# A causal and a full attention stage: the row of maxima sent from ScalarE's queue, and PSUM banks shared out two, two and two in place of three, three and one

## The chip, the cores and the metric

The kernel runs on one core of one Trainium2 chip. The metric is the device time of one execution in microseconds (us). TensorE (PE) multiplies, VectorE (DVE) reduces and does element-wise work, ScalarE (ACT) does exponentials and copies out of PSUM, GpSimd (POOL) does element-wise work on SBUF, and SyncE (SP) does nothing but issue DMAs. PSUM has eight banks of 128 partitions by 512 fp32 values.

## The reference

Four layers follow each other on x of shape (8, 512, 128): causal attention with rotary embedding and an output projection, a mixture-of-experts FFN, full attention with rotary embedding, and a dense FFN; each is added to x and followed by a layer norm. Only the two attentions are touched. Cut to what matters:

```python
qkv = x @ Wqkv                                    # 16 heads of 8 values, 512 positions, 8 batches
Q, K = rope(q), rope(k)
scores = einsum('bhqd,bhkd->bhqk', Q, K) / sqrt(8)   # causal in the first attention, full in the second
attn = softmax(scores, axis=-1)                      # exp(score - row maximum) / sum
y = einsum('bhqk,bhkd->bhqd', attn, V)
x = layernorm(x + y @ Wproj)                         # the second attention has no projection
```

## The kernel before, in words

`attention` is called twice. Its work is cut into 32 groups n = 0..31 of four heads (four groups to a batch b = n // 4, t = n % 4), and each group into units u: 12 units in the causal stage (three tiles of four heads), 16 in the full one. In every unit PE does `scores(n, u)` (L505) into a bank `ps_s`, then `maxima(n + 2, u)` (L518) for the group two ahead into a bank `ps_m`, the transposed product from which the row maxima come. Scores and maxima use 25 and 24 of the array's rows, and head i of the scores lies at other rows than the head (i + 2) % 4 of the maxima. ACT takes the exponential of each score unit out of `ps_s` (L433), DVE reduces each unit of maxima out of `ps_m` (L597 causal, L600 full). In odd units PE also does `values` (L533, the product with V), and after four of them in a group `warm` (L459), which multiplies into the bank of the next score unit only to keep PE busy. Small jobs (`job`, L468: transposing x, projecting k, q and v, transposing maxima `maxT`, normalising `norm`, and in the causal stage `yT` and `proj`) stand at fixed units and share the banks `ps_x` in a ring: a job waits until the job that last had its bank has been read.

Banks are numbered in turn: unit g = n * U + u has score bank g % SB and maxima bank g % MB. PE therefore waits in `scores` and `warm` for the exponential SB units back and in `maxima` for the reduction MB units back:

```python
after(pe, s_exp, g - SB + 1)      # scores: unit g; warm: g is the unit after this one
after(pe, s_mx, g - MB + 1)       # maxima
```

The score of a group subtracts the row's maximum through an extra row of the stacked operand `qst`. ACT copies the transposed maxima to `mrow` (L417, once a group, after unit 4 in the causal stage and unit 2 in the full one), and SP sends that row by a DMA into `qst` (`max_row`, L313). `scores(n, 0)` waits for it. SP also sends `stack(b)` (L295), 24 DMAs of 64 KB that build the stacked operands `kst` and `qst` of a batch from `hi_k`, `lo_k`, `hi_q`, `lo_q` (the rotated k and q in two parts, made by POOL, L346 and L352). `maxima(4 * b, 0)` waits for all 24. All queues run in the written order. On SP, stack(b + 1) comes behind the row of group 4b + 1, and the row of group 4b + 2 behind stack(b + 1).

Of the kernel before, what the change touches and what calls it, by code (L numbers as in the profile page):

```python
# [4 lines left out]
F32 = mybir.dt.float32  # L5
# [6 lines left out]
P = 128  # L12
C = 128
B, T = 8, 512
QT = T // P
# [3 lines left out]
NG = H // HG  # L19
PARTS = 3  # L20
QUAD = 32
KROWS = 3 * D
# [212 lines left out]
def attention(nc, sems, x, x_dram, ident, maskw, weights, wproj, cos, sin, tag, ahead=None):  # L235
# [3 lines left out]
    sh = Shapes(causal)  # L239
    U = sh.units  # L240
    G = B * NG
    SB, MB, XB = 3, 3, 1
    START = [("xT", 0), ("k", 0), ("q", 0), ("v", 0), ("xT", 1), ("k", 1), ("q", 1), ("maxT", 0)]
    END = [("norm", G - 1)] + ([("yT", B - 1), ("proj", B - 1)] if causal else [])
    place = sh.ring(START, END, XB)
# [1 line left out]
    with ExitStack() as ctx:  # L247
# [3 lines left out]
        def sbuf(name, shape, dt=F32):  # L251
            return ctx.enter_context(nc.sbuf_tensor(tag + name, shape, dt))


        qst = [sbuf(f"qst{r}", [P, NG, T], F32R) for r in range(2)]
# [10 lines left out]
        mrow = [sbuf(f"mrow{i}", [HG * QT, P], F32R) for i in range(2)]  # L266
# [17 lines left out]
        s_made, s_read, s_swap, s_turn, s_hi, s_lo = sems.made, sems.read, sems.swap, sems.turn, sems.hi, sems.lo  # L284
        s_kst, s_qst, s_mst, s_den, s_res, s_ln = sems.kst, sems.qst, sems.mst, sems.den, sems.res, sems.ln
# [6 lines left out]
        with nc.Block() as block:  # L292
            @block.sync
            def _(sp):
                def stack(b):  # L295

                    r = b % 2
                    if b >= 2:
                        sp.wait_ge(s_score, (b - 1) * NG * U)
                    for name, dst, s_dst, hi_rows, lo_rows in (("k", kst[r], s_kst[r], (D, 2 * D), (0,)),  # L300
                                                               ("q", qst[r], s_qst[r], (0, D), (2 * D,))):
                        sp.wait_ge(s_hi[name], b + 1)
                        for i in range(HG):
                            for row in hi_rows:
                                sp.dma_start(dst[QUAD * i + row:QUAD * i + row + D, :, :].bitcast(F32),
                                             hi[name][QUAD * i:QUAD * i + QUAD, :].bitcast(F32)).then_inc(s_dst, 16)
                        sp.wait_ge(s_lo[name], b + 1)
                        for i in range(HG):
                            for row in lo_rows:
                                sp.dma_start(dst[QUAD * i + row:QUAD * i + row + D, :, :].bitcast(F32),  # L310
                                             lo[name][QUAD * i:QUAD * i + QUAD, :].bitcast(F32)).then_inc(s_dst, 16)

                def max_row(n):  # L313

                    b, t = divmod(n, NG)
                    sp.wait_ge(s_read["maxT"], n + 1)
                    sp.dma_start(qst[b % 2][KROWS:P:QUAD, t, :].bitcast(F32).rearrange("i (j q) -> i j q", j=QT),
                                 mrow[n % 2][:, :].bitcast(F32)).then_inc(s_mst, 16)

                if causal:  # L320
                    for b in range(B):
                        sp.dma_start(x[:, QT * b:QT * b + QT, :], x_dram[b]).then_inc(s_load[b], 16)
                sp.wait_ge(s_ones, 2)
                stack(0)
                max_row(0)
                if ahead is not None:
                    ahead(sp)
                for n in range(G):
                    if n + 1 < G:
                        max_row(n + 1)  # L330
                    if n % NG == 0 and n // NG + 1 < B:
                        stack(n // NG + 1)

            def rope(eng, b, name, step):

# [20 lines left out]
            def _(pool):  # L356
# [9 lines left out]
                def hide(n, j):  # L366

                    k, (col, _) = sh.tile_of[j], sh.piece_of[j]
                    pool.wait_ge(s_exp, n * U + (k + 1) * HG)
                    diag = prob[k][:, :, col:col + P]  # L370
                    pool.affine_select(out=diag, in_=diag, compare_op=ALU.is_ge, fill=0.0, base=0,  # L371
                                       pattern=[[0, HG], [1, P]], channel_multiplier=-1).then_inc(s_mask, 1)
# [19 lines left out]
            @block.scalar  # L392
            def _(act):
                def read_out(name, n):

                    act.wait_ge(s_made[name], n + 1)
                    ps_x = ps_j[place[name, n][0]]
                    if name == "xT":
                        if n:
                            act.wait_ge(s_made["v"], n)  # L400
                        ins = act.activation(xT[:, :], ps_x[:, :], ACT.Copy)
                    elif name in "kq":
                        if n:
                            act.wait_ge(s_swap[name], n)
                            act.wait_ge(s_turn[name], 3 * n)
                        ins = act.activation(raw[name][:, :], ps_x[:, :], ACT.Copy)
                    elif name == "v":
                        if n < 2:
                            act.wait_ge(s_vinit, 4)
                        else:  # L410
                            act.wait_ge(s_pv, (n - 1) * NG * QT)
                        ins = act.activation(vst[n % 2][:, :, :, 0:D],
                                             ps_x[:, :].rearrange("p (j h d) -> p j h d", j=QT, h=H), ACT.Copy)
                    elif name == "maxT":
                        if n >= 2:
                            act.wait_ge(s_mst, (n - 1) * 16)
                        ins = act.activation(mrow[n % 2][:, :], ps_x[0:HG * QT, 0:P], ACT.Copy, scale=-1.0)  # L417
                    else:
                        assert name == "yT"
                        if n:  # L420
                            act.wait_ge(s_made["proj"], n)
                        ins = act.activation(yT[:, :], ps_x[:, :], ACT.Copy)
                    ins.then_inc(s_read[name], 1)

                def exponentials(n, u):

                    k, i = divmod(u, HG)
                    g = n * U + u
                    w = sum(w for _, _, w in sh.score[k])
                    act.wait_ge(s_score, g + 1)  # L430
                    if i == 0 and n:
                        act.wait_ge(s_pv, sh.tile_free(n - 1, k))
                    act.activation(prob[k][:, i, 0:w], ps_s[g % SB][:, 0:w], ACT.Exp, scale=float(D) ** -0.5)\  # L433
                        .then_inc(s_exp, 1)

                def out_read(n):

                    act.wait_ge(s_pv, (n + 1) * QT)
                    if n:
                        act.wait_ge(s_made["norm"], n)  # L440
                    act.activation(oT[:, :], ps_o[:, :], ACT.Copy).then_inc(s_oT, 1)  # L441

                for name, n in START:
                    read_out(name, n)
                for n in range(G):
                    for u in range(U):
                        exponentials(n, u)
                        if u == sh.out_at and n:
                            out_read(n - 1)
                        for name, m in sh.behind(n, u, 1):  # L450
                            if name not in ("norm", "proj"):
                                read_out(name, m)
                out_read(G - 1)
                if causal:
                    read_out("yT", B - 1)
# [1583 lines left out]
```

## Time and profile before

| | us |
|---|---|
| median of 3 runs (lowest, highest) | 1502.93 (1495.87, 1503.41) |
| the profiled execution | 1501.69 |
| its span, first to last instruction | 1500.0 |
| PE busy in the span | 1239.8 (83%) |
| DVE, ACT, POOL busy | 921.8, 788.9, 521.6 |
| mean granted TensorE clock | 0.891 of 2.4 GHz |

The causal stage lies between about 14 and 480 us of the span, the full one between about 720 and 1210. PE's instructions run in order and several matmuls on different rows of the array can be under way at once, so a busy PE is not PE at its peak. Where PE is the engine that the others wait for, a wait of PE moves the end by as much.

### The profile page before, as it was taken

The page shows a single profiled execution, that of the slowest core. Times are in us where ns is not written, and L with a number is a line of the kernel's source. Part 1 is how long each engine was busy: PE and PEld are TensorE (multiplying, and loading weights), DVE is VectorE, ACT ScalarE, POOL GpSimd, SP SyncE. Part 2 cuts the span into 40 slices and gives each one's busy share as a digit, 9 for nine tenths or more (in the row PEclk, how much of TensorE's full clock was granted, in tenths as well). Part 3 has the DMA queues.
Part 4 walks back from the last instruction along what each step waited for, and adds up shares of the span by engine and source line. Part 5 has one row for each costly group of instructions (what it writes and reads, how often), then busy time and mean ns, then how long its engine had stood idle before and what let it go on. Part 6 is the DMA issues. An engine that isn't in the chain of part 4 may idle for free. (4 is left out here: it accounts for less than half of the span.)

```text
span 1500.0 us, 28689 instructions
## 1 busy us (share of the span) xinstructions
PE 1239.8 (83%) x10443; PEld 726.8 (48%) x10443; DVE 921.8 (61%) x2838; ACT 788.9 (53%) x1543; POOL 521.6 (35%) x476
## 2 busy tenths in 40 slices
PE   3588977877798597794399899899898969999996
PEld 1344434434454464672144344343343447888885
DVE  3556855866673766445388788788787642334542
ACT  1144644644554663443137676676676745556553
POOL 3324523532511455573513033033030004445553
PEclk9988977988878598897559899999999989999998
DMA  4212113202300401333340310310321000000000
GB/s 101 29 39 45 28 18 44 34 13 44 44 2 2 130 15 41 109 62 66 42 108 15 44 34 12 44 36 11 44 31 15 2 15 8 15 14 14 14 21 15
DMA packets 55948, 53.26 MB, mean 36 GB/s; under 512 B 8000, under 2 KB 38720, under 8 KB 55824
## 3 DMA queue, kind: packets, MB, share of 16 engines
q1 hardware_dynamic: 51808, 48.33, 16.2%
q0 software_dynamic: 3696, 2.76, 1.3%
q8 instruction: 77, 1.26, 0.4%
q14 instruction: 47, 0.39, 0.1%
q10 hardware_dynamic: 320, 0.52, 0.1%
HBM read 15.74 MB, written 8.06 MB: 16 GB/s over the span
## 5 line engine op out<-in xcount | busy, mean ns | idle before, releaser
L433 ACT ACTIVATE a_prob<-a_ps_s 128x512 f32<-128x512 f32 (+1 forms) x896 | 466.4, 565 | 340.3 <-PE a_ps_s L514 336.1
L600 DVE TENSOR_REDUCE a_mx<-a_ps_m 128x1 f32<-128x512 f32 x512 | 327.9, 682 | 87.7 <-PE a_ps_m L529 86.3
L529 PE MATMUL a_ps_m<-a_kst,a_qst 24*128 24x512 f32 (+3 forms) x1024 | 284.1, 480 | 43.8 <-DMA a_qst<-a_lo_q 36.8
L597 DVE CUSTOM_DVE_ANT_0 a_junk<-a_ps_m,maskw 128x384 f32<-128x384 f32 (+3 forms) x512 | 227.2, 486 | 148.6 <-PE a_ps_m L529 148.5
L514 PE MATMUL a_ps_s<-a_qst,a_kst 25*128 25x512 f32 (+3 forms) x1024 | 246.4, 464 | 76.9 <-DMA a_qst<-a_mrow 67.4
L551 PE MATMUL a_ps_o<-a_prob,a_vst 128*32 128x256 f32 (+2 forms) x3840 | 286.6, 387 | 2.9 <-ACT a_oT L441 2.1
L514 PEld LDWEIGHTS a_ps_s<-a_qst,a_kst 25*128 25x128 f32 x1024 | 110.9, 193 | 230.8 <-ACT a_prob L433 95.7
L371 POOL TENSOR_SCALAR_AFFINE_SELECT a_prob<-a_prob 128x512 f32<-128x512 f32 x128 | 80.1, 638 | 265.6 <-ACT a_prob L433 265.6
L465 PE MATMUL a_ps_s<-a_kst 128*32 128x256 f32 x2000 | 169.8, 414 | 0.0
L529 PEld LDWEIGHTS a_ps_m<-a_kst,a_qst 24*128 24x128 f32 x1024 | 129.1, 200 | 72.1 <-issue 40.4
L551 PEld LDWEIGHTS a_ps_o<-a_prob,a_vst 128*32 128x32 f32 x3840 | 86.8, 113 | 106.4 <-issue 71.2
L338 POOL TENSOR_TENSOR a_rot_k<-a_rot_k,sin_table 128x512 f32<-128x512 f32 x16 | 20.5, 1279 | 286.3 <-DVE a_rot_k L608 286.3
L1698 POOL TENSOR_TENSOR f_hid_lo<-f_gelu_h,f_hid_hi 128x512 fp32r<-128x512 f32 x64 | 83.2, 1300 | 101.1 <-ACT f_hid_hi L1661 101.1
L1736 PE MATMUL f_ps_h<-f_hid_hi,f_h_hi 128*128 128x512 f32 x256 | 103.4, 404 | 4.0 <-POOL f_hid_lo L1698 4.0
L1738 PE MATMUL f_ps_h<-f_hid_lo,f_h_hi 128*128 128x512 f32 x256 | 101.4, 396 | 0.0
L1737 PE MATMUL f_ps_h<-f_hid_hi,f_h_lo 128*128 128x512 f32 x256 | 100.6, 393 | 0.0
L1698 POOL TENSOR_TENSOR f_hid_lo<-f_gated_h,f_hid_hi 128x512 fp32r<-128x512 f32 x32 | 41.5, 1298 | 154.7 <-ACT f_hid_hi L1650 153.9
L465 PEld LDWEIGHTS a_ps_s<-a_kst 128*32 128x32 f32 x2000 | 68.7, 119 | 35.4 <-issue 7.3
L1833 DVE SCALAR_TENSOR_TENSOR f_u<-f_th,f_ps_a 128x512 f32<-128x512 f32 x32 | 21.8, 683 | 56.3 <-ACT f_th L1645 56.3
L1736 PEld LDWEIGHTS f_ps_h<-f_hid_hi,f_h_hi 128*128 128x128 f32 x256 | 48.6, 190 | 15.8 <-POOL f_hid_lo L1698 6.4
L1738 PEld LDWEIGHTS f_ps_h<-f_hid_lo,f_h_hi 128*128 128x128 f32 x256 | 48.6, 190 | 11.2
L1737 PEld LDWEIGHTS f_ps_h<-f_hid_hi,f_h_lo 128*128 128x128 f32 x256 | 48.7, 190 | 10.0
(292 smaller groups left out, 1933.2 us busy)
## 6 DMA issues: line engine op xcount, KB each, us to landing
a_kst<-a_hi_k SPq DMA_DIRECT2D x128, 64.0 KB
a_qst<-a_hi_q SPq DMA_DIRECT2D x128, 64.0 KB
f_w<-in_L_ffn_W_dram SPq DMA_DIRECT2D x21, 256.0 KB, 3.6
a_kst<-a_lo_k SPq DMA_DIRECT2D x64, 64.0 KB
a_qst<-a_lo_q SPq DMA_DIRECT2D x64, 64.0 KB
x_tiles<-in_L_attn_x_dram SPq DMA_DIRECT2D x8, 256.0 KB, 4.6
normed_rows_dram<-f_nrm SPq DMA_DIRECT2D x8, 256.0 KB, 2.3
f_hT_hi<-expert_sums_dram SPq DMA_DIRECT2D x4, 512.0 KB, 6.0
```

What stands on the lines that cost most here:

```text
L371: pool.affine_select(out=diag, in_=diag, compare_op=ALU.is_ge, fill=0.0, base=0, pattern=[[0, HG], [1, P]], channel_multiplier=-1).then_in ...
L433: act.activation(prob[k][:, i, 0:w], ps_s[g % SB][:, 0:w], ACT.Exp, scale=float(D) ** -0.5)\
L465: pe.matmul(ps_s[g % SB][VW * i:VW * i + VW, 0:2 * P], kst[r][:, t, VW * i:VW * i + VW].bitcast(F32), kst[r][:, t, 0:2 * P].bitcast(F32), ...
L514: last = pe.matmul(ps_s[g % SB][:, col:col + w], kst[r][lo_row:end, t, P * j:P * j + P], qst[r][lo_row:end, t, T - w:T], start=True, stop= ...
L529: last = pe.matmul(ps_m[g % MB][:, col:col + w], qst[r][lo_row:end, t, P * j:P * j + P], kst[r][lo_row:end, t, 0:w], start=True, stop=True)
L551: last = pe.matmul(ps_o[VW * i:VW * i + VW, end - w:end], vst[b % 2][:, j, HG * t + i, :], prob[k][:, i, col + at:col + at + w], start=(j ...
L597: ins = dve.tensor_tensor_reduce(junk[g % MB][:, col:col + w], bank[:, col:col + w], maskw[:, T - w:T], 1.0, -3.0e38, ALU.add, ALU.max, out)
L600: ins = dve.reduce_max(out, bank[:, col:col + w], AX.X)
L1698: pool.tensor_tensor(dst, src[:, :], hi.bitcast(F32), ALU.subtract).then_inc(s_lo, 1)
L1736: pe.matmul(out, w_hi[w][:, k, cols], hi, start=start, stop=False)
L1737: pe.matmul(out, w_lo[w][:, k, cols], hi, start=False, stop=False)
L1738: return pe.matmul(out, w_hi[w][:, k, cols], lo, start=False, stop=stop)
```

## The change

The DMA of the row of maxima is issued by ACT, right behind ACT's copy that makes it, in place of SP. The wait in front of it, for ACT's own copy, moves with it. SP's queue then holds only loads and stacks, so stack(b + 1) follows stack(b) and its own waits. The seven banks beside `ps_o` are shared out as 2 for scores, 2 for maxima and 2 for small jobs (six in all), in place of 3, 3 and 1. Work and order on PE, DVE and POOL are otherwise the same.

```diff
-    SB, MB, XB = 3, 3, 1
+    SB, MB, XB = 2, 2, 2
...
-                def max_row(n):
-
-                    b, t = divmod(n, NG)
-                    sp.wait_ge(s_read["maxT"], n + 1)
-                    sp.dma_start(qst[b % 2][KROWS:P:QUAD, t, :].bitcast(F32).rearrange("i (j q) -> i j q", j=QT),
-                                 mrow[n % 2][:, :].bitcast(F32)).then_inc(s_mst, 16)
...
                 stack(0)
-                max_row(0)
                 if ahead is not None:
                     ahead(sp)
-                for n in range(G):
-                    if n + 1 < G:
-                        max_row(n + 1)
-                    if n % NG == 0 and n // NG + 1 < B:
-                        stack(n // NG + 1)
+                for b in range(1, B):
+                    stack(b)
...
                     ins.then_inc(s_read[name], 1)
+                    if name == "maxT":
+                        b, t = divmod(n, NG)
+                        act.wait_ge(s_read["maxT"], n + 1)
+                        act.dma_start(qst[b % 2][KROWS:P:QUAD, t, :].bitcast(F32).rearrange("i (j q) -> i j q", j=QT),
+                                      mrow[n % 2][:, :].bitcast(F32)).then_inc(s_mst, 16)
```

What stood in SP's queue before, in the causal stage (`kst` and `qst` are the stacked operands, `mrow` the row of maxima, x8 a run of eight DMAs):

```order
L317 DMA a0_qst1<-a0_mrow0 4x4x128
L317 DMA a0_qst1<-a0_mrow1 4x4x128
L305 DMA a0_kst0<-a0_hi_k 8x4x512 x8
L310 DMA a0_kst0<-a0_lo_k 8x4x512 x4
L305 DMA a0_qst0<-a0_hi_q 8x4x512 x8
L310 DMA a0_qst0<-a0_lo_q 8x4x512 x4
L317 DMA a0_qst1<-a0_mrow0 4x4x128
L317 DMA a0_qst1<-a0_mrow1 4x4x128
```

And what stands there after:

```order
L305 DMA a0_kst1<-a0_hi_k 8x4x512 x8
L310 DMA a0_kst1<-a0_lo_k 8x4x512 x4
L305 DMA a0_qst1<-a0_hi_q 8x4x512 x8
L310 DMA a0_qst1<-a0_lo_q 8x4x512 x4
L305 DMA a0_kst0<-a0_hi_k 8x4x512 x8
L310 DMA a0_kst0<-a0_lo_k 8x4x512 x4
```

Before, the third row of a batch stood behind the 24 DMAs of the next batch's stack, and that stack behind the second row. No row is left on SP.

What stood in ACT's queue before, from the last units of a group to the copy of the row (`prob` is the exponential, `ps_s0` to `ps_s2` the score banks):

```order
L433 ACTIVATE a0_prob0<-a0_ps_s0 128x512 [waits a_pv,a_score]
L433 ACTIVATE a0_prob0<-a0_ps_s1 128x512 [waits a_score]
L433 ACTIVATE a0_prob0<-a0_ps_s2 128x512 [waits a_score]
L433 ACTIVATE a0_prob0<-a0_ps_s0 128x512 [waits a_score]
L433 ACTIVATE a0_prob1<-a0_ps_s1 128x512 [waits a_pv,a_score]
L417 ACTIVATE a0_mrow1<-a0_ps_x0 16x128 [waits a_mst,a_made_maxT]
```

And after:

```order
L427 ACTIVATE a0_prob0<-a0_ps_s0 128x512 [waits a_pv,a_score]
L427 ACTIVATE a0_prob0<-a0_ps_s1 128x512 [waits a_score]
L427 ACTIVATE a0_prob0<-a0_ps_s0 128x512 [waits a_score]
L427 ACTIVATE a0_prob0<-a0_ps_s1 128x512 [waits a_score]
L427 ACTIVATE a0_prob1<-a0_ps_s0 128x512 [waits a_pv,a_score]
L406 ACTIVATE a0_mrow1<-a0_ps_x1 16x128 [waits a_mst,a_made_maxT]
L416 DMA a0_qst1<-a0_mrow1 4x4x128 [waits a_read_maxT]
L427 ACTIVATE a0_prob1<-a0_ps_s1 128x512 [waits a_score]
```

The score banks repeat after two units, the small jobs have banks `ps_x0` and `ps_x1`, and the DMA stands between the copy and the exponential of the next unit.

## Rows read from the trace of the kernel before

**Rows 1.** The waits: engine, line, releaser; us in total, times, longest.
```profile
ACT a_prob L433 <- PE a_ps_s L514: 336.1, 311, 12.3
PEld a_ps_s L514 <- ACT a_prob L433: 95.7, 207, 0.8
PE a_ps_s L514 <- DMA a_qst<-a_mrow: 67.4, 14, 7.2
```
**Rows 2.** The timeline of SP in batch 2: start, us, line, DMAs in a run.
```profile
172.82 5.69 SPq L305 DMA_DIRECT2D a_kst<-a_hi_k  x8
...
189.90 37.47 SPq L317 DMA_DIRECT2D a_qst<-a_mrow  x4
```
**Rows 3.** The timeline of PE: the first scores behind the wait of that batch.
```profile
198.41 0.79 PE L514 MATMUL a_ps_s<-a_qst,a_kst 25*128 25x512 f32 x1 [7.18 <-DMA a_qst<-a_mrow]
```
**Rows 4.** Windows: stretch, length, busy PE, PEld, DVE, ACT, POOL; PEclk, DMA share, GB/s.
```profile
155.00:160.00 5.00, 3.63 (x48) 1.49 (x38) 3.53 (x13) 1.72 (x5) 0.89 (x2) 1.00 0.00 0
187.00:188.00 1.00, 1.00 (x9) 0.46 (x13) 1.00 (x7) 0.00 (x0) 0.64 (x1) 0.50 0.52 68
196.00:197.00 1.00, 0.00 (x0) 0.00 (x0) 0.00 (x0) 0.00 (x0) 0.00 (x0) 0.50 0.31 27
203.00:204.00 1.00, 1.00 (x11) 0.19 (x4) 1.00 (x6) 0.44 (x1) 0.49 (x1) 0.59 0.00 0
```
**Rows 5.** The timeline of ACT: copies of the row of maxima, and the exponential behind one.
```profile
171.91 0.25 ACT L417 ACTIVATE a_mrow<-a_ps_x 16x128 fp32r<-16x128 f32 x1
181.46 0.25 ACT L417 ACTIVATE a_mrow<-a_ps_x 16x128 fp32r<-16x128 f32 x1
181.62 0.57 ACT L433 ACTIVATE a_prob<-a_ps_s 128x512 f32<-128x512 f32 x1
205.02 0.25 ACT L417 ACTIVATE a_mrow<-a_ps_x 16x128 fp32r<-16x128 f32 x1
```
**Rows 6.** The timeline of PE in the causal stage, first units of a group.
```profile
158.09 0.49 PE L514 MATMUL a_ps_s<-a_qst,a_kst 25*128 25x512 f32 x1
159.20 0.61 PE L465 MATMUL a_ps_s<-a_kst 128*32 128x256 f32 x8
159.74 0.49 PE L514 MATMUL a_ps_s<-a_qst,a_kst 25*128 25x512 f32 x1
160.42 0.61 PE L465 MATMUL a_ps_s<-a_kst 128*32 128x256 f32 x8
```
**Rows 7.** The timeline of ACT and DVE in the same stretch.
```profile
158.61 0.60 ACT L433 ACTIVATE a_prob<-a_ps_s 128x512 f32<-128x512 f32 x1 [3.28 <-PE a_ps_s L514]
158.76 0.69 DVE L597 CUSTOM_DVE_ANT_0 a_junk<-a_ps_m,maskw 128x512 f32<-128x512 f32 x1 [1.44 <-PE a_ps_m L529]
159.37 0.08 DVE L597 DVE_READ_ACCUMULATOR2_ANT a_mx<- 128x1 f32 x1
159.37 0.69 DVE L597 CUSTOM_DVE_ANT_0 a_junk<-a_ps_m,maskw 128x512 f32<-128x512 f32 x1
```
**Rows 8.** The timeline of PE in the full stage: warming and bare pairs.
```profile
860.72 0.49 PE L514 MATMUL a_ps_s<-a_qst,a_kst 25*128 25x512 f32 x1
861.61 0.61 PE L465 MATMUL a_ps_s<-a_kst 128*32 128x256 f32 x8
...
869.18 0.50 PE L514 MATMUL a_ps_s<-a_qst,a_kst 25*128 25x512 f32 x1
...
870.18 0.50 PE L514 MATMUL a_ps_s<-a_qst,a_kst 25*128 25x512 f32 x1
```
**Rows 9.** The timeline of SP: the first row's DMA alone.
```profile
61.92 0.57 SPq L317 DMA_DIRECT2D a_qst<-a_mrow  x1
```
**Rows 10.** The timeline of POOL: `hi_k` and `hi_q` of batch 3.
```profile
166.06 1.27 POOL L346 TENSOR_TENSOR a_hi_k<-a_full_k,a_rot_k 128x512 fp32r<-128x512 f32 x1
175.71 1.28 POOL L346 TENSOR_TENSOR a_hi_q<-a_full_q,a_rot_q 128x512 fp32r<-128x512 f32 x1
```
**Rows 11.** Groups of instructions: one of the small jobs.
```profile
L481 PE MATMUL a_ps_x<-a_xT,heads_k 128*128 128x512 f32 x32 | 21.7, 765 | 10.0 <-DVE a_y L620 6.9 <-ACT a_xT L401 3.1
```

## What the change was predicted to do

> **What bounds the kernel now.** I read the waits first, then the timelines of SP, PE, ACT and DVE around the longest wait, and the windows for the clock. In both attention stages ACT waits 336.1 us for PE's scores, while PE's own long waits are few [rows 1]. So PE sets the pace, and each delay of PE there counts in full. One kind of wait stands out: PE waits 14 times, 67.4 us in all, for the row of maxima [rows 1]. It comes once a batch. In batch 2 SP issues the stack from 172.82, gets to the row at 189.90, and PE goes on at 198.41 after 7.18 us idle [rows 2, 3]. Traffic goes on until about 197 [rows 4], so the row waited for SP's 17 us of issuing and then behind the stack's data in the queue. ACT had made the row at 181.46 [rows 5]. The clock makes it dearer: it stands at 0.50 (1.2 GHz) from 187 and is back at 2.4 GHz only within 203 to 204 [rows 4]. From copy to copy of the row a group takes 9.55 us (171.91 to 181.46), but the one with the wait takes 23.56 (to 205.02) [rows 5].
>
> The other thing to see is how tightly PE and ACT mesh even with three banks: the weight load of a score unit stands 207 times, 95.7 us in all, in front of an exponential that isn't done, never over 0.8 us [rows 1]. The spare bank isn't idle.
>
> **Term 1, the row's own wait: a gain of 57 us.** The row leaves ACT at about 181.7 + 0.6 in batch 2, 10 us before PE wants it at 191.23 (198.41 less 7.18). Its wait goes. What is late next is the stack: the maxima of group 4b + 2 wait for all 24 DMAs. Their data ended at about 197, and the stack began at 172.82. In the changed kernel it begins when hi_k is there and the last batch's scores are done, at about 167.4 (166.06 + 1.27 [rows 10]), 5.4 us earlier. Its second half needs hi_q, ready at 176.99 [rows 10]. 24 DMAs took 21.5 us of traffic (from about 175), so 12 take 10.8; the first twelve are through at about 180, the last at about 191 and their signal a us or two later. PE comes at 191.2, so 1.5 us is left of a wait of 7.18 in a causal batch. In the full stage groups are longer and little is left. I take 7 x 1.5, some 10 us, off 67.4. The bounds are 0 left (gain 67) and 1.8 us of each gained (5.4 less 3.6, half the head start lost to hi_q: gain 25).
>
> **Term 2, the slow clock behind these waits: a gain of 19 us.** The group with the wait took 23.56 us; with its extra v job it should take 10.6 (9.55 [rows 5] and an estimated 1.1 for the job). Of the 13.0 lost, 7.2 are the wait [rows 3] and 5.8 the slow running around it. There are seven such batches in the causal stage, most with somewhat less: 38 us at 5.4 each. Bounds: 0 (the clock falls anyway: in batch 2 it was down at 187 [rows 4], before the wait began at 191) and 38. I take the middle. In the full stage, where the clock is up until the wait starts, I count nothing.
>
> **Term 3, two banks for small jobs: a gain of 9 us.** A job then waits for the reader of the job before last. The 6.9 us of the k projection behind DVE's normalising [rows 11] and some 2 us of shorter ones go. In the start-up, where a job waits 0.7 us for each read-out, the stack's DMAs follow anyway. Bounds 3 to 13.
>
> **Term 4, two score and two maxima banks: a loss of 117 us.** The unit of work on PE is a pair of units: four matmuls (scores and maxima of both) start within 0.02 us of each other, since they lie at different rows of the array, and take 0.43 us before the next kind starts. Take a causal pair that starts at 158.09. Its first exponential starts at 158.61 and takes 0.60 [rows 7], so the bank is free 1.17 after the pair's start (0.52 + 0.60 + 0.05). ACT's next follows 0.48 later, and frees its bank at 1.65. DVE's first reduction starts at 158.76, the second at 159.37, and that ends at 0.69 + 0.08 more [rows 7]: second maxima bank free at 2.05 to 2.1.
> With three banks the warming unit waits for none of these. With two it waits for the first exponential of its own pair, the next first score for the same one, the next second score for the second exponential, and the next second maxima for the second reduction.
> - Warming (four a group in either stage) starts 1.11 after the pair in one case and 0.68 in the next (159.20 and 160.42 against 158.09 and 159.74) [rows 6]. In place of that 1.2: losses 0.1 and 0.5. The third of a causal group stands behind as much `values` work as the first but shorter columns (an estimated 0.3), the fourth behind exponentials of half the width (0). Together 0.9. In the full stage all four are like 861.61 against 860.72, 0.89 [rows 8]: 0.3 each, 1.2.
> - Second reduction: the next pair follows at 1.66 (159.74) [rows 6], after the loss above at about 1.75 to 2.0, and its second maxima may start only at 2.05. A pair without warming is the worse: 1.00 from 869.18 to 870.18 [rows 8]. There the first maxima wait until 1.3, the second until 1.9. The pair is then staggered by 0.6, no longer four at once, and the next values and warming come later by as much. That is 0.9 for a bare pair, one a causal group (with a 0.3 at the group's end where the normalising stands before DVE's last reduction), one or two a full group. 0.9 + 0.3 less what overlaps with the first item gives 1.0 in the causal stage; 1.0 in the full one, where a job in the pair covers the stagger in half of them.
> Together 1.9 a group causal, 2.0 full (1.2 + 1.0 less 0.2 for pairs with a long job), over 30 groups each: 57 + 60 = 117 us. Bounds: 45 us where only warming and half of it counts (0.75 a group), and 165 us at 2.75 a group with every stagger passed on.
>
> **Term 5, the DMA on ACT: a loss of 30 us.** The next exponential starts 0.16 after ACT's copy (181.46, 181.62) [rows 5]. Now the copy must end (0.25, and 0.05 for the signal) and the DMA be issued; on SP one took 0.57 [rows 9]. The trace shows no such DMA on ACT beside exponentials. The next exponential starts about 0.7 later (0.27 + 0.57 less 0.16). It is the second of its pair, whose bank with two banks is waited for: free at about 2.4 instead of 1.65. Of this 0.7 about 0.5 isn't covered by term 4, 60 times: 30 us. Bounds: 0 (ACT gets so far ahead that nobody waits) and 42. Queued behind it are the exponentials, and for them PE waits.
>
> Sum: 1501.7 for the profiled execution - 57 - 19 - 9 + 117 + 30 = 1563.7. The profiled execution lies 1.2 us under the median of 1502.93, so the forecast of the median is 1565 us, 4.1% slower.
>
> **Rivals.**
> - A, faster: the third banks are a reserve that the pair's rhythm doesn't need. Place: the pairs of every group. It speaks for it that no wait for an exponential is over 0.8 us [rows 1] and that ACT is idle between its pairs. Then terms 4 and 5 are at their lower ends, 45 and 0: 1501.7 - 57 - 38 - 9 + 45 = 1444. It decides once the banks cost under 1.4 us a group (85 / 60). Against it: the 207 waits, and the exponential's end at 1.17 is later than three of four warmings.
> - B, the clock: each pair now has a PE gap of 0.3 to 0.5 us. In 155 to 160 PE was busy 3.63 of 5 us and the clock stayed at 1.00; in batch 2 it was down at 187, four us before the long idle time began [rows 3, 4]. So it stands near the edge, and groups of 9.6 us with 2.4 more idle may go over it. At 1.2 GHz the same matmul took 0.79 instead of 0.49 [rows 3, 6], so a pair of 1.66 takes 2.65 or so. Against the new 1.9 that is 0.75 more; in 60 of the 180 causal pairs 45 us, and term 2 is lost: 1565 + 45 + 19 = 1629.
> - C, the wait moves: the stack lands no earlier than PE wants it, since hi_q and the queue hold its second half. Term 1 is then 25 and term 2 zero: 1565 + 32 + 19 = 1616. It speaks against it that the causal groups get longer, which gives the stack 4 us more.
> The Trainium skill, "TensorE: Matmul & The Clock Gate", section "A second HAM failure mode: psum-queue depth-cycling", tells of a kernel that cycled through PSUM banks and whose short gaps made the clock swing between its two levels. By that, rival B is what would happen here; the trace bears it out only so far as the clock that was down at 187.
>
> **How the numbers follow.** Forecast 0.5, A 0.17, B 0.18, C 0.15. The forecast's own range, with one of the large terms at half its distance to a bound, is 1525 to 1600. A range for 8 in 10 leaves out the better half of A and the worst of B: 1470 to 1630. A measurement of this kernel tells about 0.5% (7.5 us) from no change. Faster by more: A but for its tail, and a bit of the forecast's, 0.15; within: 0.05; slower: 0.80.
>
> **What the changed profile would show.** Right: no wait of PE for the row; a wait of the maxima for lo_q of 0 to 3 us in causal batches only; SP's stacks from about 5 us earlier; waits for exponentials and reductions in hundreds, PE's before warming and second maxima; copies of the row 11.5 to 12 us apart where they were 9.55; the exponential behind the copy 0.8 us after it. Wrong: spacing still near 9.6 (A), PEclk at 0.50 away from the batch's end (B), maxima waiting 4 us or more for lo_q (C). A spacing that grows in the causal stage but not in the full one would make the term of the bare pairs wrong.

## The result, and the profile after

The changed kernel is slower by 10%: 1653.47 us (median of 4 runs, 1644.02 to 1661.73) against 1500.82 us of the kernel before (4 runs, 1495.87 to 1503.41) on the same chip. The ratio is 1.1019, 95% interval 1.0941 to 1.1098. The prediction was 1565 us with a range of 1470 to 1630. The direction was right, and the loss was two and a half times the one forecast. Where times and ratios stand side by side below, a time is the median of all executions, and a ratio leaves out one execution each of runs 3 and 5 that took over 1.5% longer than the fastest of the same kernel.

The page of the changed kernel, its first part and the clock line:
```profile
PE 1398.4 (84%) x10443; PEld 764.5 (46%) x10443; DVE 939.0 (57%) x2838; ACT 807.7 (49%) x1543; POOL 521.3 (31%) x476
...
PEclk8588887889876888985599889888797857999998
```
The matmuls are the same 10443 as before, but PE is busy for 1398.4 us where it was 1239.8, 13% more. Part of that is slower running: the score matmuls take 497 ns on average instead of 464, and the clock line has 8s and 7s also in the second attention stage (slices 21 to 32), where before most slices stood at 9. The other part is that matmuls which used to run at the same time now start one after another (windows of 7 and 8 below); busy time counts them apart.

Next the waits of the changed kernel (columns as in [rows 1]):
```profile
ACT a_prob L427 <- PE a_ps_s L508: 439.4, 427, 10.4
...
PEld a_ps_s L508 <- ACT a_prob L427: 150.8, 262, 1.2
...
PE a_ps_m L523 <- DMA a_qst<-a_lo_q: 51.7, 2, 26.6
PEld a_ps_s L459 <- ACT a_prob L427: 51.1, 139, 0.6
PE a_ps_s L508 <- ACT a_prob L427: 49.7, 91, 0.9
...
PEld a_ps_m L523 <- DVE a_mx L594: 38.6, 71, 1.5
...
PE a_ps_s L508 <- DMA a_qst<-a_mrow: 6.6, 2, 4.3
```
The row's wait is gone but for the start of the two stages: 67.4 us in 14 waits [rows 1] have become 6.6 in 2. In its place stand hundreds of waits, none long, of score and warming units for exponentials and of maxima for reductions. The weight load alone waits 150.8 us for exponentials (95.7 before, [rows 1]). The maxima wait for `lo_q` only at the two stage starts, and longer there than before (51.7 us for 36.8).

The stack of batch 3 in SP's timeline, and ACT's copies 9 to 11 (counted from 0) with what stands behind one:
```profile
181.85 6.87 SPq L305 DMA_DIRECT2D a_kst<-a_hi_k  x8
```
```profile
187.94 0.25 ACT L406 ACTIVATE a_mrow<-a_ps_x 16x128 fp32r<-16x128 f32 x1
188.22 0.54 ACTq L416 DMA_DIRECT2D a_qst<-a_mrow  x1
188.81 1.09 ACT L427 ACTIVATE a_prob<-a_ps_s 128x512 f32<-128x512 f32 x2 [0.62 <-ACT a_mrow L406]
...
200.67 0.25 ACT L406 ACTIVATE a_mrow<-a_ps_x 16x128 fp32r<-16x128 f32 x1
...
216.85 0.25 ACT L406 ACTIVATE a_mrow<-a_ps_x 16x128 fp32r<-16x128 f32 x1
```
The stack begins 6.1 us before copy 9, the second one of the batch under way; before, it began 0.9 us after that copy (172.82 against 171.91, [rows 2, 5]). The exponential stands 0.87 behind the copy's start, where it was 0.16 [rows 5]. The group from 200.67 to 216.85 takes 16.18 us where it took 23.56. Groups without a batch's end take longer: 11.68 (176.26 to 187.94) against 9.65, and 12.73 against 9.55. The first of these two runs at full clock, the second at a mean of 0.87.

Last, windows (columns as in [rows 4]). First the kernel before: its full stage, from the copy of row 0 to that of row 31, and its causal stage from 100 us on:
```profile
763.29:1187.46 424.17, 392.33 (x4092) 169.80 (x4092) 352.28 (x757) 289.62 (x569) 76.12 (x60) 0.94 0.20 35
...
100.00:464.75 364.75, 306.32 (x3672) 165.08 (x3672) 244.18 (x1142) 188.19 (x422) 145.04 (x172) 0.86 0.19 28
```
And of the changed kernel: the full stage, the causal stage from 100 us, two single groups of the full stage, a piece of the first of them, and the 33 us behind the full stage's last copy:
```profile
803.54:1330.70 527.16, 485.77 (x4091) 194.52 (x4091) 362.79 (x757) 301.50 (x570) 75.95 (x60) 0.85 0.14 21
...
100.00:494.02 394.02, 360.49 (x3753) 176.52 (x3751) 250.89 (x1158) 196.83 (x429) 145.18 (x173) 0.85 0.16 26
...
1086.60:1105.65 19.05, 18.10 (x145) 7.51 (x141) 12.55 (x31) 10.04 (x20) 0.04 (x1) 0.73 0.53 70
1105.65:1121.07 15.42, 13.35 (x137) 5.64 (x133) 12.40 (x33) 9.57 (x19) 0.00 (x0) 1.00 0.01 3
...
1089.00:1092.00 3.00, 3.00 (x26) 0.89 (x18) 1.43 (x3) 1.94 (x4) 0.00 (x0) 0.50 0.54 71
...
1330.70:1364.00 33.30, 32.98 (x204) 11.57 (x196) 1.10 (x4) 16.17 (x31) 0.00 (x0) 0.50 0.01 1
```
By stage, the span grew by some 157 us: 3 before the first copy, 26 in the causal stage, 11 between the stages, 103 in the full stage, 15 behind it. The full stage is where the forecast failed most. It holds clean groups of 15.4 us at full clock (the second of the two) beside groups of 17 to 20 us; in the first of the two the clock averages 0.73, so for half its time it was at 0.50 (1.2 GHz). Between 1089 and 1092 PE looks 100% busy. It isn't doing more, each matmul takes longer:
```profile
1086.76 0.49 PE L508 MATMUL a_ps_s<-a_qst,a_kst 25*128 25x512 f32 x1
...
1088.12 0.50 PE L508 MATMUL a_ps_s<-a_qst,a_kst 25*128 25x512 f32 x1 [0.74 <-ACT a_prob L427]
...
1089.06 1.10 PE L459 MATMUL a_ps_s<-a_kst 128*32 128x256 f32 x8
1090.09 0.79 PE L508 MATMUL a_ps_s<-a_qst,a_kst 25*128 25x512 f32 x1
```
This is PE's timeline in the group whose row was copied at 1086.60. A score unit waits 0.74 us for the exponential that ACT's DMA had delayed, and within a microsecond of that wait the warming unit takes 1.10 where it took 0.61, and the score matmul 0.79 in place of 0.50.

The trace records the granted clock as a list of stretches. Its first entry lies at 77 us of the span in the kernel before, at 24 in the changed one, so stretches are added up from 100 us of the span to its end: at 0.50 stand 27 stretches with 318 us before, and 56 with 473 us after.

### The profile page after: what moved, and what is told of

Same layout as the page of the kernel before. It is cut to its first block and busy times, and to the rows that moved or that the text cites. A ratio compares the mean times of both kernels' runs of the same rounds, so it can differ in the third digit from the quotient of the medians.

```text
span 1657.9 us, 28687 instructions
## 1 busy us (share of the span) xinstructions
PE 1398.4 (84%) x10443; PEld 764.5 (46%) x10443; DVE 939.0 (57%) x2838; ACT 807.7 (49%) x1543; POOL 521.3 (31%) x476
## 5 line engine op out<-in xcount | busy, mean ns | idle before, releaser
L427 ACT ACTIVATE a_prob<-a_ps_s 128x512 f32<-128x512 f32 (+1 forms) x896 | 475.2, 568 | 464.4 <-PE a_ps_s L508 439.4
L594 DVE TENSOR_REDUCE a_mx<-a_ps_m 128x1 f32<-128x512 f32 x512 | 338.1, 687 | 184.8 <-PE a_ps_m L523 184.0
L523 PE MATMUL a_ps_m<-a_kst,a_qst 24*128 24x512 f32 (+3 forms) x1024 | 361.4, 502 | 72.2 <-DMA a_qst<-a_lo_q 51.7
L508 PE MATMUL a_ps_s<-a_qst,a_kst 25*128 25x512 f32 (+3 forms) x1024 | 310.5, 497 | 59.5 <-ACT a_prob L427 49.7
L545 PE MATMUL a_ps_o<-a_prob,a_vst 128*32 128x256 f32 (+2 forms) x3840 | 319.2, 424 | 0.0
L508 PEld LDWEIGHTS a_ps_s<-a_qst,a_kst 25*128 25x128 f32 x1024 | 134.8, 204 | 266.5 <-ACT a_prob L427 150.8
L523 PEld LDWEIGHTS a_ps_m<-a_kst,a_qst 24*128 24x128 f32 x1024 | 156.6, 207 | 112.7 <-issue 53.3
L459 PE MATMUL a_ps_s<-a_kst 128*32 128x256 f32 x2000 | 186.0, 449 | 9.8 <-ACT a_prob L427 4.4
L459 PEld LDWEIGHTS a_ps_s<-a_kst 128*32 128x32 f32 x2000 | 60.2, 123 | 87.6 <-ACT a_prob L427 51.1
L486 PE MATMUL a_ps_x<-ident,a_oT 128*128 128x128 f32 x256 | 52.6, 340 | 1.6 <-ACT a_oT L435 1.6
```

Source lines behind the costliest of these rows:

```text
L459: pe.matmul(ps_s[g % SB][VW * i:VW * i + VW, 0:2 * P], kst[r][:, t, VW * i:VW * i + VW].bitcast(F32), kst[r][:, t, 0:2 * P].bitcast(F32), ...
L508: last = pe.matmul(ps_s[g % SB][:, col:col + w], kst[r][lo_row:end, t, P * j:P * j + P], qst[r][lo_row:end, t, T - w:T], start=True, stop= ...
L523: last = pe.matmul(ps_m[g % MB][:, col:col + w], qst[r][lo_row:end, t, P * j:P * j + P], kst[r][lo_row:end, t, 0:w], start=True, stop=True)
L545: last = pe.matmul(ps_o[VW * i:VW * i + VW, end - w:end], vst[b % 2][:, j, HG * t + i, :], prob[k][:, i, col + at:col + at + w], start=(j ...
L594: ins = dve.reduce_max(out, bank[:, col:col + w], AX.X)
```

## The experiments

Each ratio is to runs of the kernel before on the same chip (median 1498.71 us for 1 to 4, 1495.75 for 5 to 8, 1498.93 for 9 and 10). "Low clock" is the sum of the stretches at 0.50 from 100 us on, in the profiled execution; those of 3 and 5 were the longest of their four (1570.51 and 1615.25 us). "Banks s, m, x" are the score, maxima and small-job banks.

| | banks | row issued by | time, us | ratio (95%) | low clock, us |
|---|---|---|---|---|---|
| before | 3,3,1 | SP | 1500.82 | 1 | 318 |
| 1 | 3,3,1 | ACT | 1449.93 | 0.9682 (0.9645 to 0.9719) | 210 |
| 2 | 2,2,2 | SP | 1630.00 | 1.0900 (1.0856 to 1.0944) | 413 |
| 3 | 3,2,2 | ACT | 1552.98 | 1.0343 (1.0268 to 1.0418) | 333 |
| 4 | 2,3,2 | ACT | 1577.66 | 1.0559 (1.0501 to 1.0616) | 340 |
| 5 | 2,2,2 and one for warming | ACT | 1600.28 | 1.0667 (1.0612 to 1.0723) | 398 |
| 6 | as 5, more warming | ACT | 1575.10 | 1.0513 (1.0472 to 1.0555) | 227 |
| 7 | 2,2,2 | GpSimd | 1597.18 | 1.0691 (1.0642 to 1.0740) | 333 |
| 8 | 3,3,1 | GpSimd | 1434.79 | 0.9591 (0.9527 to 0.9656) | 221 |
| 9 | 2,2,1 | ACT | 1649.28 | 1.1018 (1.0966 to 1.1071) | 446 |
| 10 | 3,3,1, half stack held | GpSimd | 1429.75 | 0.9506 (0.9468 to 0.9544) | 235 |
| after | 2,2,2 | ACT | 1653.47 | 1.1019 (1.0941 to 1.1098) | 473 |

**1: the moved row alone.** The changed kernel with
```
-    SB, MB, XB = 2, 2, 2
+    SB, MB, XB = 3, 3, 1
```


> The row's DMA on ScalarE's queue as in the changed kernel, banks 3, 3, 1 as before. Theory (the banks are the loss, the moved row a gain): PE's 14 waits for the row (67 us) go, some slow clock with them, and ACT's DMA is hidden by the third bank, so 1420 to 1460 us, ratio to before about 0.96, copies of the row 9.5 to 10 us apart in the causal stage. Rival (the DMA on ScalarE's queue is the loss): 1530 us or more, since its 0.7 us stands in all 64 groups and the stack's wait takes the place of the row's.

1449.93 us, as the theory had it: this half of the change is a gain of 49 us. The rows of the full stage, and two of its copies, one group apart:
```profile
720.34:1137.71 417.37, 392.08 (x4092) 164.92 (x4092) 353.81 (x757) 290.11 (x570) 76.08 (x60) 0.96 0.18 28
```
```profile
949.88 0.25 ACT L406 ACTIVATE a_mrow<-a_ps_x 16x128 fp32r<-16x128 f32 x1
...
963.01 0.25 ACT L406 ACTIVATE a_mrow<-a_ps_x 16x128 fp32r<-16x128 f32 x1
```
The clock holds at 0.96. The group takes 13.13 us; the same one took 12.52 before. So ACT's DMA costs 0.6 a full group even with three banks.

**2: the banks alone.** The kernel before with the same line at 2, 2, 2.

> Banks 2, 2, 2 as in the changed kernel, the row's DMA on SyncE's queue as before. Theory: the waits for the row stay (14, about 60 us) and the banks cost their full price, so slower than the changed kernel: 1680 to 1720 us. Rival (the DMA on ScalarE's queue is the loss): 1530 to 1580, faster than the changed kernel's 1653.

1630.00, between the two theories. The banks alone cost 131 us, and with them the row's move loses 23 where with three it gains 49: the edits don't add. One reason stands in the waits of this kernel:
```profile
PE a_ps_s L514 <- DMA a_qst<-a_mrow: 12.3, 5, 2.9
```
PE waits less for the row where groups are longer; of 67.4 us [rows 1] only 12.3 are left to be gained. The other reason is what ACT's DMA costs between two banks (7).

**3 and 4: one bank given back.** The changed kernel with `SB, MB, XB = 3, 2, 2`, and with `2, 3, 2`.

> The changed kernel with a third score bank (3, 2, 2). Theory: warming and the second score unit no longer wait for the pair's own exponentials and the DMA on ScalarE is covered, but the maxima still wait for the reduction two units back. I put 60 per cent of the banks' price on the score bank: about 1530 us. Rival (the maxima bank is the dear one): 1600 or more.

> The changed kernel with a third maxima bank (2, 3, 2). Theory: the second maxima and the stagger behind them no longer wait, 40 per cent of the banks' price comes back: about 1570 us, with waits for exponentials as in the changed kernel. Rival (the maxima bank is the dear one): 1510 or less.

1552.98 and 1577.66. From the changed kernel, a third score bank gives 100 us and a third maxima bank 76, of the 203 that lie between 1 and the changed kernel. Each result lies nearer its theory (1530, 1570) than its rival. Both kinds matter, the scores more.

**5 and 6: warming in a bank of its own, and then more of it.** The warming matmuls' result is never read; in 5 they go to the eighth, free bank and wait for nothing:
```
-                    after(pe, s_exp, g - SB + 1)
...
-                        pe.matmul(ps_s[g % SB][VW * i:VW * i + VW, 0:2 * P], kst[r]...
+                        pe.matmul(ps_v[VW * i:VW * i + VW, 0:2 * P], kst[r]...
```
6 adds warming units in front of the small jobs, one a causal group and four a full one:
```
+                        if u in ((7,) if causal else (3, 7, 11, 15)) and (n, u) != (G - 1, U - 1):
+                            warm(n, u)
```


> The changed kernel, with the warming matmuls going to the eighth bank, which the changed kernel leaves free, so that they wait for no exponential; same work. Theory: my 0.9 us (causal) and 1.2 us (full) a group for the warming's wait come back in part, since the second maxima then wait instead; about 30 to 50 us of 1653, so 1605 to 1625, and the waits of the warming for exponentials vanish. Rival (all that counts is the second reduction): no change, 1645 to 1660.

> As the run before, with more warming matmuls in the spare bank: also in the pairs that had none (unit 7 in the causal stage, units 3, 7, 11 and 15 in the full one), 8 more instructions of some 0.55 us in all each time, 150 times. Theory (the clock's falls make up the rest of the loss): falls of the clock go from 58 to 25 or fewer and, as the added work lies in gaps, the time is 20 us or more under the run before, 1590 or less. Rival (the waits alone make up the loss, the clock does little): the added work of 0.55 x 150 = 80 us is half hidden and the time is 30 us or more over the run before.

1600.28 and 1575.10. No wait of warming for an exponential is left in 5, and the time is 53 us lower, just under the expected range. The full stage of 5, then of 6:
```profile
778.48:1287.20 508.72, 466.84 (x4091) 196.57 (x4091) 363.22 (x757) 300.86 (x569) 76.02 (x60) 0.88 0.15 22
```
```profile
755.33:1260.12 504.79, 475.95 (x5055) 213.83 (x5059) 364.86 (x757) 301.13 (x570) 76.02 (x60) 0.96 0.15 23
```
6 runs 964 more matmul records in that stage and is still shorter. The clock there goes from 0.88 to 0.96, and the low stretches of the whole kernel from 398 us in 47 stretches to 227 in 23 (473 in 56 in the changed kernel). The profiled execution of 5 was its longest, but its four executions were granted 0.858 to 0.877 and those of 6 0.909 to 0.914, so the difference doesn't hang on it. The gaps between the pairs pull the clock down, and filling them brings it back. This is the run that shows the clock as a cause and not a by-product: only the filler was added, and it can't shorten a group by itself. At full clock it costs: the cleanest four groups of the full stage take 15.48, 15.15, 15.56 and 15.36 us in 5 and 16.76, 16.18, 15.97 and 15.95 in 6, some 0.8 more each, or 26 us over 31 groups. The stage is 4 us shorter all the same, so by this estimate about 30 us came back from the clock there.

**7 and 8: the row on GpSimd.** The DMA is taken out of ACT's small job and issued by POOL, once a group, with a semaphore of its own in each attention; 7 has banks 2, 2, 2 and 8 has 3, 3, 1:
```
+                def max_row(n):
+                    b, t = divmod(n, NG)
+                    pool.wait_ge(s_read["maxT"], n + 1)
+                    pool.dma_start(qst[b % 2][KROWS:P:QUAD, t, :]..., mrow[n % 2]...).then_inc(s_mst, 16)
```


> The changed kernel with the row's DMA issued by GpSimd in place of ScalarE, banks 2, 2, 2. Theory (the DMA holds up the second exponential of a pair, and with two banks that is passed on): 0.5 to 0.6 us a group over 62 groups and the clock falls that go with it, 30 to 60 us: 1595 to 1625. Rival (the DMA on ScalarE costs nothing): 1645 to 1660.

> Banks 3, 3, 1 with the row's DMA issued by GpSimd. With the row on ScalarE the full stage's groups were 13.1 and 13.7 us apart instead of 12.5 and 13.1. Theory: that 0.6 us goes in about 60 groups, 25 to 37 us: 1412 to 1425, and the groups are 12.5 and 13.1 apart. Rival (GpSimd gets to its DMA late, behind its rotations and masks): waits for the row come back and the time is 1450 or more.

1597.18, as the theory had it, and 1434.79, over the expected 1412 to 1425, though the groups are 12.5 and 13.1 apart as forecast. ACT's DMA costs 56 us with two banks and 15 with three; the 15 is the weaker number, since the intervals of 1 and 8 overlap a little, but the full stage of 8 (400.93 us against 417.37) and its groups (12.54 against 13.13) say the same. With two banks the profiled executions are 69 us apart, and 51 of these lie in the full stage, whose row in 7 reads:
```profile
793.85:1270.18 476.33, 454.59 (x4091) 190.49 (x4091) 360.58 (x757) 299.48 (x569) 93.97 (x91) 0.93 0.16 24
```
against 527.16 at 0.85 with ACT's DMA. The pair 7 and 8 also gives the cleanest price of the banks. The copies of one full group in 8, and of one in 7:
```profile
944.56 0.25 ACT L416 ACTIVATE a_mrow<-a_ps_x 16x128 fp32r<-16x128 f32 x1
...
957.10 0.25 ACT L416 ACTIVATE a_mrow<-a_ps_x 16x128 fp32r<-16x128 f32 x1
```
```profile
1052.29 0.25 ACT L416 ACTIVATE a_mrow<-a_ps_x 16x128 fp32r<-16x128 f32 x1
...
1067.22 0.25 ACT L416 ACTIVATE a_mrow<-a_ps_x 16x128 fp32r<-16x128 f32 x1
```
12.54 and 14.93, so 2.4 us for this group; the causal groups between copies 8 and 9 took 9.66 and 11.65, 2.0 more. The windows of these two full groups, 8 and then 7, and of one more in 7:
```profile
944.56:957.10 12.54, 12.40 (x141) 6.08 (x141) 11.69 (x30) 9.67 (x21) 6.94 (x6) 1.00 0.54 70
```
```profile
1052.29:1067.22 14.93, 14.58 (x145) 6.73 (x141) 12.46 (x31) 9.98 (x20) 6.93 (x6) 1.00 0.54 70
882.54:897.38 14.84, 13.54 (x137) 5.83 (x133) 12.30 (x33) 9.49 (x20) 0.58 (x1) 1.00 0.16 20
```
All three run at full clock. In the same group PE is busy for 14.58 us instead of 12.40, though its matmuls average 0.40 us in both: they no longer run side by side. So a busy PE hides the gaps of the pairs.

**9: the second small-job bank.** The changed kernel with `SB, MB, XB = 2, 2, 1`.

> The changed kernel with one bank for the small jobs in place of two, all else as in it. It isolates the prediction's third term (9 us gained by the second bank, bounds 3 to 13). Theory: a job on one bank waits for the read-out of the job before, and PE idles some tenths of a us for it now and then; this kernel then takes 1656 to 1670 us, the changed one beside it 1653. Rival: with two score and two maxima banks PE waits for those anyway, and the third term's waits are hidden behind them, so that nothing changes: within 3 us of 1653, or even less if the longer queue of small jobs had made the exponentials late.

1649.28: no difference from the changed kernel (1.1018 against 1.1019). The rival was right, the second bank is worth nothing beside two score and two maxima banks. With three of each it would need a ninth bank.

**10: the first row ahead of the stack.** 8 with
```
                         sp.wait_ge(s_hi[name], b + 1)
+                        if b == 1 and name == "q":
+                            sp.wait_ge(s_read["maxT"], 1)
```


> Three score, three maxima and one small bank with the row of maxima issued on GpSimd (1435 us before), and in addition the second half (q) of batch 1's stack waits until the first row has been made, at about 62 us. Theory: at the start the first row waited for data of that stack which was in flight ahead of it (issued 62.6, PE went on at 73.4 after 6.9 us idle); with the half stack issued behind it the row lands within 2 to 3 us of its issue, PE's wait for it at the start falls from 6.9 to about 0, group 1 comes some 7 us earlier, and the stack is complete at about 75, just in time: 1425 to 1430 us. Rival 1: the wait only moves to the maxima of batch 1, which then find the stack late by as much: 1435. Rival 2: the row's own DMA takes 9 us there for another reason: PE's wait stays near 6.9.

PE's first scores of the causal stage in 8, and in this kernel:
```profile
73.41 0.79 PE L513 MATMUL a_ps_s<-a_qst,a_kst 25*128 25x512 f32 x1 [6.88 <-DMA a_qst<-a_mrow]
```
```profile
66.06 0.79 PE L515 MATMUL a_ps_s<-a_qst,a_kst 25*128 25x512 f32 x1
```
The wait is gone, and PE is 7.35 us earlier though GpSimd issued the row at the same moment (62.57 and 62.62). The next copy follows the first by 8.45 us and not 15.6. The rows show that much. They don't show a faster kernel: the last causal copy stands at 422.38 us against 422.73, and the profiled executions took 1438.72 and 1437.97, so the 7 us were lost again on the way, with 48 us of low clock in the causal stage instead of 31. The median, 1429.75, is in the expected range, but the intervals of 8 and 10 overlap a little. It is the lowest time here, 4.9% under the kernel before; that it beats 8 isn't shown.

## Why the prediction was wrong

**The step that failed** is the treatment of the clock. Term 2 says of the full stage, "where the clock is up until the wait starts, I count nothing", and terms 4 and 5 were priced from matmuls and gaps at full clock. By stage, the terms and what the two profiled executions show:

| | predicted | measured |
|---|---|---|
| causal stage | -31 - 19 - 7 + 57 + 15 = +15 | +26 |
| full stage | -26 - 2 + 60 + 15 = +47 | +103 |
| outside both | 0 | +29 |

Of the full stage's excess of 56, most is slow running. The four groups of a batch, each at its cleanest (clock 1.00 from copy to copy; some shorter groups near the stage's start and end left out), take:

| full stage, us a group | groups of a batch | mean |
|---|---|---|
| run 8 (banks 3,3,1) | 12.93, 13.12, 12.52, 13.25 | 12.96 |
| run 7 (banks 2,2,2) | 15.15, 15.35, 14.93, 14.84 | 15.07 |
| changed kernel (and DMA on ACT) | 15.78, 15.38, 15.55, 15.42 | 15.53 |

The 14.84 is the window from 882.54 shown in 7; the other groups in that place take 16.0 to 16.1 in run 7, with the clock down for part of them. So at full clock the banks cost 2.1 us a group and ACT's DMA 0.46, where the prediction had 2.0 and 0.5: 66 and 14 us over the stage's 31 groups, beside the forecast 60 and 15. 31 groups of 15.53 would be 481 us, and they took 527, so 46 us are an estimate of what the falls of the clock cost there. With the 23 us that the stage gains from the moved row (run 8 against the kernel before) that is the whole of it: -23 + 66 + 14 + 46 = 103. By the trace's list of stretches the stage was at 0.50 for 55 us before and for 158 us after. Behind the stage, the last window shows 33 us at 0.50 where the kernel before stood at 0.90; from the last copy to the end it lost 15 us. Between the stages the kernels take 298.5 us (before), 301.5 (run 1), 306.9 (run 2) and 309.5 (changed), so most of the 11 us comes with the banks.

Rival B had this mechanism, with 0.18, but priced it in the causal stage alone. There low clock rose little in sum (104 to 116 us, from 100 us on), but it is other low clock: the moved row takes most of the old stretches away (24 us left in run 1), and the banks bring new ones (102 in run 7). By the rule of the Trainium skill that the prediction cited ("TensorE: Matmul & The Clock Gate", "A second HAM failure mode: psum-queue depth-cycling") the clock was to swing, and the traces agree (27 stretches, then 56); the page tells it of a bf16 kernel and gives no size.

Term by term, in medians, in the order row, banks, ACT, from runs 8, 7 and the changed kernel:

| | predicted | measured |
|---|---|---|
| row off SP's queue (terms 1 and 2) | -76 | -61 (1495.8 to 1434.8) |
| second small-job bank (term 3) | -9 | 0 (run 9) |
| two score and two maxima banks (term 4) | +117 | +162 (1434.8 to 1597.2) |
| DMA on ACT (term 5) | +30 | +56 (1597.2 to 1653.5) |

The misses are 15 + 9 + 45 + 26 = 95 us, less 7 because the kernel before ran at 1495.8 beside runs 7 and 8: the 88 between 1565 and 1653. In another order the parts read otherwise: banks +131, row -33, ACT +56.

**Terms 1 and 2** held in mechanism. The wait for the row went, the stack started early, no maxima of a batch waited for it. By the profiles of the kernel before and run 8 the causal stage gains 42 us (forecast 50), the full one 23 (26), and 3 are lost between them. Of the 8 missing in the causal stage, 7 lie in its first group, where the row now waits behind the stack (15.60 us against 8.45).

**Term 3** was mis-sized. The 6.9 us that PE waited before the k projection [rows 11] are gone in run 9 too, with one small-job bank, so the two score and maxima banks cover them. At the stage starts the second bank only moves a wait: PE waits 51.7 us for `lo_q` with it and 38.5 without.

**Term 4** was right at full clock: 2.1 us a full group for the 2.0, and 2.0 for the 1.9 in the causal group that can be compared. By the profiles of 8 and 7 the stages grow by 61 us (causal, predicted 57) and 75 (full, 60, of which 66 at full clock). That the causal 61 comes so near is partly luck, since it holds slow running that the term left out (102 us of low clock for 31). So with the spacing: copies that were 9.65 apart are 11.68 apart, in the forecast 11.5 to 12, but those that were 9.55 apart, which the forecast named, are 12.7 to 14.3 apart, at a clock of 0.87 or 0.76. Another 17 us lie outside the stages, where no term was, and the last 9 between these profiled executions and the medians. One small piece that the working left out: DVE's last step of the layer norm stands ahead of reductions, and with two banks PE waits for them (22 waits for reductions in the full stage, 12.0 us in all). In the full stage of the changed kernel, DVE and then PE:
```profile
1115.28 1.11 DVE L72 TENSOR_SCALAR x_tiles<-x_tiles,a_mv,a_rs 128x128 f32<-128x128 f32 x4
1116.29 1.96 DVE L594 TENSOR_REDUCE a_mx<-a_ps_m 128x1 f32<-128x512 f32 x3
```
```profile
1117.04 0.49 PE L523 MATMUL a_ps_m<-a_kst,a_qst 24*128 24x512 f32 x1 [1.11 <-DVE a_mx L594]
```

**Term 5** was right at full clock: the exponential is late by the forecast amount, and a full group pays 0.46 us for it, 14 us in the stage for the forecast 15. But the stage lost 51 us by it. The other 37 are the clock's: the gap of 0.74 us comes on top of the banks' gaps, and without it run 7's full stage had 63 us at low clock for the 158. In the causal stage it cost 7.

**Rivals.** A fell: spacing left 9.6 at once, and giving up the third banks cost more than forecast, not less. C fell: no maxima of a batch waited for `lo_q`. B was right as a mechanism, and its sign came true: the clock now falls away from the batch's end, in the causal stage too. Its 1629 is nearer to 1653 than the forecast, but by luck: it put +79 us into the causal stage, which grew by 26, and nothing for the clock into the full one.

## What to carry to other kernels

When an edit adds many short gaps on TensorE, price them a second time for the clock, in the stage that looks safest: PE was 92% busy in the full stage both before and after, at a clock of 0.94 and 0.85. Its busy share can't warn you, since matmuls that no longer run side by side fill it. Two edits that lean on the same reserve don't add: a DMA issue of 0.54 us on ScalarE cost 15 us with three banks and 56 with two. Put a small transfer on an engine that nobody waits for, and look at what traffic is in flight ahead of it, not only at the queue that issues it.

## What the hardware showed that was not expected

A queue of its own didn't carry the small row past transfers that another engine had already issued. At the start of the changed kernel ACT issued it at 65.01, three microseconds after SP's last stack DMA, and PE could use it at 74.58. ACT's and PE's rows, and the windows between:
```profile
65.01 0.61 ACTq L416 DMA_DIRECT2D a_qst<-a_mrow  x1
```
```profile
74.58 0.79 PE L508 MATMUL a_ps_s<-a_qst,a_kst 25*128 25x512 f32 x1 [4.29 <-DMA a_qst<-a_mrow]
```
```profile
70.00:72.00 2.00, 0.29 (x1) 0.00 (x0) 0.51 (x4) 0.00 (x0) 0.00 (x0) 0.50 0.54 66
72.00:74.00 2.00, 0.00 (x0) 0.00 (x0) 0.00 (x0) 0.00 (x0) 0.00 (x0) 0.50 0.22 27
74.00:76.00 2.00, 0.80 (x4) 0.29 (x4) 0.44 (x1) 0.59 (x2) 0.00 (x0) 0.50 0.00 0
```
The row landed when the stack's traffic (share 0.54) had drained. It wasn't its signal alone that was late: by the trace's record of packets the row's own 16 packets of 512 bytes run from 72.50 to 73.97, 7.5 us and more behind the issue, and the stack's last one ends at 73.90. In run 8 the row's first data packet starts 8.4 us behind the issue on GpSimd. With half of the stack held back (run 10) its data packets start 1.4 to 1.5 us behind the issue. The Trainium skill ("DMA: Bandwidth & Descriptors", "Queues, rings and completion order") says that a DMA engine takes turns between its queue rows packet by packet. By that rule alone the row's packets should have moved within a few of the stack's; the traces show over 7 us, and the measurement decides. Where the row waited in between isn't shown.

The other surprise is run 6: work of no use to the result, put into gaps, made the kernel 25 us faster.
